# Fetching the condition indices as four packed rows and transposing them on VectorE, in a conditional FFN kernel

## The chip, the cores and the metric

The kernel runs on one core of a Trainium2 chip. The metric is the device time of one execution in microseconds (us), as the median of several runs. For the kernel before it is 79.45 us (three runs, 79.31 to 79.57). One more execution was recorded by the hardware profiler; all rows in this document come from such recordings. Engine names in rows: PE is TensorE's matmuls, PEld its weight loads, DVE is VectorE, ACT is ScalarE, POOL is GpSimd, and SPq is the queue on which SyncE issues DMAs.

## The reference, cut to what matters

```python
# x: (32, 32, 256) f32; conditions: (32,) int32; weights: (200, 32, 32)
w = weights[conditions]                          # one 32x32 matrix for each of 32 batches
y = jnp.einsum('bct,bcd->bdt', x, w)             # the mixing
h = jax.nn.silu(jnp.einsum('bsh,hi->bsi', y, w_gate)) * jnp.einsum('bsh,hi->bsi', y, w_up)
h_sparse = _sparsify_2to4(h)                     # keep the two largest of every four by magnitude
out = x + jnp.einsum('bsi,ih->bsh', h_sparse, w_down)
```

The condition index of each batch picks its 32x32 matrix. Nothing can be mixed, and so nothing can go through the FFN, before those matrices are on the chip.

## The kernel before, in words

The program is written engine by engine, with semaphores set by hand, so each engine does its work in the order of the code.

**The FFN.** 32 batches are handled in two halves of four groups, each group four batches on 128 partitions. A half has 512 columns, the intermediate dimension is 1024, taken in two quarters `q` of four 128-row tiles (`M = 4`). That gives 16 pairs of a gate product and an up product (`gate_up`, line 588, over `split_product`, line 564). Every f32 product is done as three products of a high and a low part, so six 128x512 matmuls per tile. The second matrix (`down`, line 599) follows at the end of TensorE's program. ScalarE makes the high parts, silu and magnitudes; VectorE makes the low parts, the gate times up products and the comparisons of the 2-in-4 selection.

**The start, which the change touches.** SyncE issues the small array `cond` first (line 189), then the first half of x (line 191) and the first gate weights (line 192). It then waits until the first gather has landed (line 194) before it issues the rest of the gate weights, the up weights and what follows. `cond` holds for each of the 128 partitions four int32: an index for each half, and for each half the first row of the partition's chunk in the table. The table is laid out by the host as 8 chunks of 200 rows, each row 128 floats. VectorE adds the two pairs (line 456), which gives `rows_sb`, one table row per partition and half. GpSimd, which has marked `own_block` by five small memsets before (lines 220 and 223), then runs two indirect DMAs (line 226), one per half, each of 128 rows of 512 bytes into `mix_row`. VectorE transposes the 32x32 blocks of the first (`transpose_rows`, line 365) and sets `transposed`.

TensorE in the meantime runs 12 matmuls on a constant whose result nobody uses (`warm_up`, line 533). It then waits for the first high gate weights, for `transposed` and for x (line 539), and mixes the first 128 features batch by batch in 32-row matmuls (line 544), the other 128 by a block-diagonal matrix in 128-row ones (line 558). `first_gates` (line 577, matmuls on line 585) and all the rest follow.

Of the kernel before, what the change touches and what calls it, by code (L numbers as in the profile page):

```python
# [10 lines left out]
def adaln_ffn(nc: bass.Bass, x: bass.AP, x_t: bass.AP, cond: bass.AP, table: bass.AP,  # L11
# [5 lines left out]
    f32 = mybir.dt.float32  # L17
    f32r = mybir.dt.float32r
    bf16 = mybir.dt.bfloat16
    ALU = mybir.AluOpType  # L20
    ACT = mybir.ActivationFunctionType

    P = 128
    i32 = mybir.dt.int32
    _, _, GH, T = x.shape
    NH = 2
    NG = NH * GH
    C = D = 32
    D4 = D // CHUNKS
    NB = P // C  # L30
# [17 lines left out]
    with ctx:  # L48
        def sb(name, shape, dt):
            return ctx.enter_context(nc.sbuf_tensor(name, shape, dt))  # L50

        def sem(name):
            return ctx.enter_context(nc.semaphore(name))

        x_sb = sb("x_sb", [P, NG, T], f32)
        cond_sb = sb("cond_sb", [P, 2 * NH], i32)
        rows_sb = sb("rows_sb", [P, NH], i32)
        raw_w = [sb("gate_raw", [P, NQ, KT, M * P], f32), sb("up_raw", [P, NQ, KT, M * P], f32)]
        down_raw = sb("down_raw", [P, NQ, M * T], f32)
        w_hl = [sb("gate_hl", [P, 2, NQ, KT, M, P], f32r), sb("up_hl", [P, 2, NQ, KT, M, P], f32r)]  # L60
# [43 lines left out]
            return (first_in[k], 16) if w == 0 else (up_in, 16)  # L104

        cond_in = sem("cond_in")
        x_in = [sem(f"x_in{i}") for i in range(NH)]
        up_in = sem("up_in")
        rest_in = [sem(f"rest_in{w}") for w in range(2)]
# [5 lines left out]
        rows_done = sem("rows_done")  # L115
        blocks_marked = sem("blocks_marked")
# [60 lines left out]
        def parts_until(u, j):  # L177
            return sum(len(p) for p in PARTS[:u]) + 1 + max(i for i, p in enumerate(PARTS[u]) if p[0] <= j)
# [7 lines left out]
            return w_hl[w][:, part, q, k:end, j:j_end]  # L186

        def sync_program(sp):
            sp.dma_start(cond_sb[:], cond).then_inc(cond_in, 16)

            sp.dma_start(x_sb[:, 0:GH, :], x[0]).then_inc(x_in[0], 16)
            sp.dma_start(raw_w[0][:, 0, 0, 0:2 * P], w_gate[0, 0, 0]).then_inc(first_in[0], 16)

            sp.wait_ge(mix_in[0], 16)
            for k in range(1, KT):
                sp.dma_start(raw_w[0][:, 0, k, 0:2 * P], w_gate[0, 0, k]).then_inc(first_in[k], 16)
            sp.dma_start(raw_w[1][:, 0, :, 0:2 * P], w_up[0, 0].rearrange("k p n -> p k n")).then_inc(up_in, 16)
            for w, weights in enumerate((w_gate, w_up)):
                sp.dma_start(raw_w[w][:, 0, :, 2 * P:4 * P],
                             weights[0, 1].rearrange("k p n -> p k n")).then_inc(rest_in[w], 16)  # L200
            sp.wait_ge(up_in, 16)
            sp.dma_start(x_sb[:, GH:NG, :], x[1]).then_inc(x_in[1], 16)
            for w, weights in enumerate((w_gate, w_up)):
                for i in range(2):
                    sp.dma_start(raw_w[w][:, 1, :, 2 * i * P:2 * (i + 1) * P],
                                 weights[1, i].rearrange("k p n -> p k n")).then_inc(second_in[w], 16)
            sp.dma_start(down_raw[:], w_down).then_inc(down_in, 16)
            sp.wait_ge(w_hi, GATE_PIECES_END)
            sp.wait_ge(w_lo, GATE_PIECES_END)
            sp.dma_start(xt_sb, x_t).then_inc(xt_in, 16)  # L210
            for i, (half, k, begin, end, _) in enumerate(OUTPUTS):
                if i not in (UNFINISHED, LEFT):
                    cols = slice(half * TH + begin, half * TH + end)
                    sp.wait_ge(out_done, i + 1)
                    sp.dma_start(out[:, k, cols], xt_sb[:, k, cols]).then_inc(stored, 16)

            sp.wait_ge(stored, 16 * (len(OUTPUTS) - 1))

        def gpsimd_program(pool):
            nc.gpsimd.memset(own_block[:], 0.0).then_inc(blocks_marked, 1)  # L220
            pool.wait_ge(blocks_marked, 1)
            for b in range(NB):
                nc.gpsimd.memset(own_block[b * C:(b + 1) * C, b:b + 1], 1.0).then_inc(blocks_marked, 1)
            pool.wait_ge(rows_done, 1)
            for half in range(NH):
                nc.gpsimd.indirect_dma_start(
                    out=mix_row[:, half], out_offset=None, in_=table,
                    in_offset=bass.IndirectOffsetOnAxis(ap=rows_sb[:, half:half + 1], axis=0),
                    engine_sem=gather_sent,
                ).then_inc(mix_in[half], 16)  # L230

            def low_down(q):
                pool.wait_ge(down_neg, q + 1)
                pool.dma_start(down_hl[:, LO, q].rearrange("p j t -> p (j t)"), down_raw[:, q],  # L234
                               accum_op=ALU.add).then_inc(down_lo_sent[q], 16)

            def low_h(u, j, end):
                pool.wait_ge(h_neg, parts_until(u, j))
                pool.dma_start(h_hl[:, u, LO, j:end], hs[u][:, j:end],  # L239
                               accum_op=ALU.add).then_inc(h_lo_sent[u][j // 2], 16)  # L240

            low_down(0)
            low_down(1)
            for u in range(SENT):
                for j, end in PARTS[u]:
                    low_h(u, j, end)
# [108 lines left out]
        def vector_program(dve):  # L355
# [9 lines left out]
            def transpose_rows(half):  # L365
                dve.wait_ge(mix_in[half], 16)
                groups = mix_w[:, half * GH:(half + 1) * GH].rearrange("p i o d -> p (i o d)")
                nc.vector.transpose(groups.rearrange("p (r e) -> p e r", e=D4),
                                    mix_row[:, half].rearrange("p (e c) -> p e c", e=D4)).then_inc(transposed, 1)
# [75 lines left out]
            def output(i):  # L445
# [3 lines left out]
                if i > UNFINISHED:  # L449
                    dve.wait_ge(out_done, UNFINISHED + 1)  # L450
                nc.vector.tensor_tensor(xt_sb[:, k, cols], bank[:, begin:end], xt_sb[:, k, cols],  # L451
                                        ALU.add).then_inc(out_done, 1)

            dve.wait_ge(cond_in, 16)
            dve.wait_ge(blocks_marked, 1 + NB)
            nc.vector.tensor_tensor(rows_sb[:], cond_sb[:, 0:NH], cond_sb[:, NH:2 * NH], ALU.add).then_inc(rows_done, 1)
            transpose_rows(0)
            diagonal(SPANS[0])
            diagonal(SPANS[1])
# [72 lines left out]
        def tensor_program(pe):  # L532
# [106 lines left out]
            for i in range(UNFINISHED + 1, len(OUTPUTS)):  # L639
                down(LAST, i, HALVED)  # L640

        sync_program(nc.sync)
        gpsimd_program(nc.gpsimd)
        scalar_program(nc.scalar)
        vector_program(nc.vector)
        tensor_program(nc.tensor)

# [47 lines left out]
```

## Time and profile before

| | |
|---|---|
| median of 3 runs | 79.45 us (79.31 to 79.57) |
| the profiled execution, its own time | 79.29 us |
| its span, first to last instruction | 78.0 us |
| PE busy | 74.8 us, 96% of the span |
| PEld busy | 59.7 us, 77% |
| DVE busy | 62.5 us, 80% |
| ACT busy | 42.1 us, 54% |
| POOL busy | 8.1 us, 10% |
| mean HBM and SBUF traffic | 124 GB/s |

The profiled execution's time is 1.29 us above its span: that is what lies before the first instruction and after the last. The profile gives a busy time per engine, the span in 40 equal slices, and a chain, followed back from the last instruction to what released each step. Matmuls are pipelined and their ends are modelled: a matmul's record is longer than the distance to the next one's start. An idle engine costs time only where another waits for it.

### The profile page before, as it was taken

What the parts mean: (1) busy time and instruction counts of PE and PEld (TensorE: products, weight loads), DVE (VectorE), ACT (ScalarE), POOL (GpSimd) and SP (SyncE); (2) the same over time, 40 slices, a digit from 0 to 9 for tenths busy, and PEclk for the clock granted to TensorE, in tenths of its full rate; (3) what the DMA queues carried; (4) which work ended last, traced back from release to release, by engine and by line L of the source; (5) the groups of instructions that cost most, each with busy time, mean ns of one, the idle gap of its engine ahead of it and who ended that gap; (6) DMA issues with size and microseconds to landing.
All of it is one profiled execution on the core that took longest, in us unless ns stands there. A gap on an engine that the chain in (4) does not pass through costs nothing.

```text
span 78.0 us, 1015 instructions
## 1 busy us (share of the span) xinstructions
PE 74.8 (96%) x362; PEld 59.7 (77%) x362; DVE 62.5 (80%) x92; ACT 42.1 (54%) x62; POOL 8.1 (10%) x17
## 2 busy tenths in 40 slices
PE   5999999999999999999999999999999999999970
PEld 2328888888888888888888888888888888888860
DVE  0016983699789999599999979999999999996370
ACT  6122863889443375599897759879380321830000
POOL 3550000000000013000713000005300000000000
PEclk9999999999999999999999999999999999999999
DMA  0836988997920004900099990001995000002534
GB/s 1 257 113 154 327 238 285 302 417 202 361 88 21 0 0 82 187 0 0 0 202 200 202 204 13 4 0 34 202 191 111 0 0 0 8 0 75 194 134 135
DMA packets 4566, 9.64 MB, mean 124 GB/s; under 512 B 561, under 2 KB 2865, under 8 KB 4305
## 3 DMA queue, kind: packets, MB, share of 16 engines
q1 hardware_dynamic: 3488, 6.16, 23.5%
q0 software_dynamic: 928, 3.28, 22.1%
q10 hardware_dynamic: 144, 0.13, 0.5%
q8 instruction: 3, 0.05, 0.3%
q14 instruction: 3, 0.02, 0.1%
HBM read 5.38 MB, written 1.05 MB: 82 GB/s over the span
## 4 chain that ended last, share of the span: by engine, by line
PE 96%; DVE 1%; issue 0%
PE banks L573 52%; PE banks L615 28%; PE banks L535 7%; PE banks L558 4%; PE banks L585 4%; PE banks L544 1%; DVE gate_raw L451 1%
## 5 line engine op out<-in xcount | busy, mean ns | idle before, releaser
L573 PE MATMUL banks<-y_hl,up_hl 128*128 128x512 f32 x96 | 24.2, 389 | 0.0
L615 PE MATMUL banks<-h_hl,down_hl 128*128 128x512 f32 (+1 forms) x102 | 22.0, 376 | 0.0
L573 PE MATMUL banks<-y_hl,gate_hl 128*128 128x512 f32 x84 | 21.4, 390 | 0.0
L615 PEld LDWEIGHTS banks<-h_hl,down_hl 128*128 128x128 f32 x102 | 18.5, 188 | 3.6
L573 PEld LDWEIGHTS banks<-y_hl,up_hl 128*128 128x128 f32 x96 | 18.0, 188 | 3.7
L573 PEld LDWEIGHTS banks<-y_hl,gate_hl 128*128 128x128 f32 x84 | 15.7, 188 | 3.2
L262 ACT ACTIVATE silu<-banks 128x512 f32<-128x512 f32 x16 | 9.6, 597 | 11.4 <-PE banks L573 11.1
L400 DVE TENSOR_TENSOR h<-banks,silu 128x512 f32<-128x512 f32 x12 | 8.2, 687 | 4.0 <-ACT silu L262 3.9
L283 ACT ACTIVATE h_hl<-h 128x1024 fp32r<-128x1024 f32 (+1 forms) x8 | 6.7, 842 | 3.9 <-DVE h L436 3.9
L436 DVE SCALAR_TENSOR_TENSOR h<-count,h 128x512 f32<-128x512 bf16 x12 | 7.9, 685 | 0.1
L535 PE MATMUL banks<-const-bfloat16-1.0 128*128 128x512 bf16 x12 | 5.3, 627 | 0.8 <-PEq L684 0.8
L269 ACT ACTIVATE x_sb<-h 128x512 f32<-128x512 f32 x8 | 4.9, 625 | 1.7 <-DVE h L400 1.7
L451 DVE TENSOR_TENSOR gate_raw<-banks,gate_raw 128x512 f32<-128x512 f32 (+1 forms) x6 | 3.5, 599 | 2.4 <-PE banks L615 2.3
L239 POOL DMA_DIRECT2D h_hl<-h x4 | 3.7, 930 | 13.4 <-ACT h_hl L287 13.4
L234 POOL DMA_DIRECT2D down_hl<-down_raw x2 | 1.8, 920 | 31.3 <-ACT down_hl L278 31.3
L411 DVE TENSOR_TENSOR far<-x_sb 128x1024 bf16<-128x1024 f32 x4 | 4.9, 1221 | 0.2
L411 DVE TENSOR_TENSOR far<-a_even 128x1024 bf16<-128x1024 f32 x4 | 4.9, 1220 | 0.2
L535 PEld LDWEIGHTS banks<-const-bfloat16-1.0 128*128 128x128 bf16 x12 | 1.6, 140 | 3.5 <-issue 3.5
L252 ACT ACTIVATE gate_hl<-gate_raw 128x256 fp32r<-128x256 f32 (+2 forms) x4 | 2.5, 630 | 3.2 <-DMA gate_raw<-in_w_gate 3.1
L287 ACT ACTIVATE h_hl<-h 128x1024 fp32r<-128x1024 f32 x4 | 4.2, 1054 | 0.0
L283 ACT ACTIVATE h_hl<-up_raw 128x1024 fp32r<-128x1024 f32 x2 | 2.1, 1054 | 3.2 <-DVE up_raw L436 3.2
L389 DVE TENSOR_TENSOR y_hl<-banks,y_hl 128x512 fp32r<-128x512 f32 (+1 forms) x3 | 2.6, 867 | 0.9 <-ACT y_hl L256 0.8
(38 smaller groups left out, 66.2 us busy)
## 6 DMA issues: line engine op xcount, KB each, us to landing
h_hl<-h POOLq DMA_DIRECT2D x4, 512.0 KB, 6.1
x_sb<-in_x SPq DMA_DIRECT2D x2, 512.0 KB, 4.3
up_raw<-in_w_up SPq DMA_DIRECT2D x4, 256.0 KB, 4.5
down_raw<-in_w_down SPq DMA_DIRECT2D x1, 1024.0 KB, 8.0
gate_raw<-in_x_t SPq DMA_DIRECT2D x1, 1024.0 KB, 7.3
down_hl<-down_raw POOLq DMA_DIRECT2D x2, 512.0 KB, 4.8
gate_raw<-in_w_gate SPq DMA_DIRECT2D x3, 256.0 KB, 4.2
out<-gate_raw SPq DMA_DIRECT2D x3, 256.0 KB, 2.3
```

What stands on the lines that cost most here:

```text
L239: pool.dma_start(h_hl[:, u, LO, j:end], hs[u][:, j:end], accum_op=ALU.add).then_inc(h_lo_sent[u][j // 2], 16)
L262: nc.scalar.activation(silu[:, n % 3], gate_bank(n), ACT.Silu).then_inc(silu_done, 1)
L269: nc.scalar.activation(a[u % 2][:, j], hs[u][:, j], ACT.Abs).then_inc(abs_done, 1)
L283: nc.scalar.activation(h_hl[:, u, HI, j:end], hs[u][:, j:end], ACT.Copy).then_inc(h_hi, 1)
L287: nc.scalar.activation(h_hl[:, u, LO, j:end], hs[u][:, j:end], ACT.Copy, scale=-1.0).then_inc(h_neg, 1)
L400: nc.vector.tensor_tensor(hs[u][:, j], up_bank(n), silu[:, n % 3], ALU.mult).then_inc(h_done, 1)
L411: step(nc.vector.tensor_tensor(far[:, j - 2::2], au[:, 0:2], au[:, j:j + 1].broadcast_to([P, 2, TH]), ALU.is_ge))
L436: nc.vector.scalar_tensor_tensor(hs[u][:, j], count[:, j], bound, hs[u][:, j], op, ALU.mult).then_inc(masked, 1)
L451: nc.vector.tensor_tensor(xt_sb[:, k, cols], bank[:, begin:end], xt_sb[:, k, cols], ALU.add).then_inc(out_done, 1)
L535: nc.tensor.matmul(gate_bank(0), ones[:, 0:P], ones, start=True, stop=True)
L573: last = nc.tensor.matmul(dst, w_hl[w][:, s, q, k, j], y_hl[:, m, half, k], start=i == 0, stop=i == len(terms) - 1)
L615: last = nc.tensor.matmul(bank[:, begin:end], down_hl[:, s, q, j, k * P:(k + 1) * P], h_hl[:, u, m, j, begin:end], start=(q, j, m, s) == f ...
```

## The change

The host now packs `cond` into four rows, one for each group of 32 partitions: 32 indices of the first half, 32 of the second, and 32 first rows of chunks, 96 int32 (384 bytes) per row. The DMA writes them to partitions 0, 32, 64 and 96. As the other partitions of that tile would hold what was there before, VectorE first clears the whole tile, and SyncE waits for that before it issues any DMA. When the rows are in, VectorE adds the first rows to both halves' indices (64 sums per partition, of which only those on the four partitions mean something), waits for the sums, and transposes a 128x32 tile of them per half in 32x32 blocks, so that column 0 of each block column holds the table row of each partition. GpSimd waits for each half's transpose before that half's gather.

```diff
-        cond_sb = sb("cond_sb", [P, 2 * NH], i32)
-        rows_sb = sb("rows_sb", [P, NH], i32)
+        cond_sb = sb("cond_sb", [P, (NH + 1) * C], i32)
+        sums_sb = sb("sums_sb", [P, NH * C], i32)
+        rows_sb = sb("rows_sb", [P, NH * C], f32)
...
         def sync_program(sp):
-            sp.dma_start(cond_sb[:], cond).then_inc(cond_in, 16)
+            sp.wait_ge(cond_clear, 1)
+            sp.dma_start(cond_sb[0:P:C], cond).then_inc(cond_in, 16)
 
             sp.dma_start(x_sb[:, 0:GH, :], x[0]).then_inc(x_in[0], 16)
...
-            pool.wait_ge(rows_done, 1)
             for half in range(NH):
+                pool.wait_ge(rows_done, half + 1)
                 nc.gpsimd.indirect_dma_start(
                     out=mix_row[:, half], out_offset=None, in_=table,
-                    in_offset=bass.IndirectOffsetOnAxis(ap=rows_sb[:, half:half + 1], axis=0),
+                    in_offset=bass.IndirectOffsetOnAxis(ap=rows_sb[:, half * C:half * C + 1].bitcast(i32), axis=0),
...
+            nc.vector.memset(cond_sb[:], 0).then_inc(cond_clear, 1)
+            dve.wait_ge(blocks_marked, 1 + NB)
             dve.wait_ge(cond_in, 16)
-            dve.wait_ge(blocks_marked, 1 + NB)
-            nc.vector.tensor_tensor(rows_sb[:], cond_sb[:, 0:NH], cond_sb[:, NH:2 * NH], ALU.add).then_inc(rows_done, 1)
+            halves = cond_sb.rearrange("p (f r) -> p f r", r=C)
+            nc.vector.tensor_tensor(sums_sb.rearrange("p (f r) -> p f r", r=C), halves[:, 0:NH],
+                                    halves[:, NH:NH + 1].broadcast_to([P, NH, C]), ALU.add).then_inc(rows_summed, 1)
+            dve.wait_ge(rows_summed, 1)
+            for half in range(NH):
+                nc.vector.transpose(rows_sb[:, half * C:(half + 1) * C],
+                                    sums_sb[:, half * C:(half + 1) * C].bitcast(f32)).then_inc(rows_done, 1)
             transpose_rows(0)
...
-    cond = _np.concatenate([cond, first], axis=-1).reshape(P, 2 * NH)
+    cond = _np.concatenate([cond, first[..., :1]], axis=-1).reshape(NB, P // NB, NH + 1).transpose(0, 2, 1).reshape(NB, -1)
```

VectorE's queue at the start of the program, before: the ISA row is the add of the indices, the STREAM_TRANSPOSE the one of the gathered rows.

```order
L456 ISA rows_sb<-cond_sb 128x4 [waits barrier_Pool_Activation_PE_DVE_SP_release,blocks_marked,cond_in]
L368 STREAM_TRANSPOSE h<-h 128x4x32 [waits mix_in0]
L376 TENSOR_TENSOR h<-h,own_block 128x256 [waits transposed] x2
L382 TENSOR_TENSOR gate_hl<-gate_raw,gate_hl 128x256 [waits first_in0,w_hi]
L389 TENSOR_TENSOR y_hl<-banks,y_hl 128x512 [waits mixed,y_hi]
```

And the same place in the change, where the first line of the gathered rows is L373:

```order
L459 MEMSET cond_sb 128x96 [waits barrier_Pool_Activation_PE_DVE_SP_release]
L463 ISA sums_sb<-cond_sb 128x128 [waits cond_in,blocks_marked]
L467 STREAM_TRANSPOSE rows_sb<-sums_sb 128x32 [waits rows_summed]
L467 STREAM_TRANSPOSE rows_sb<-sums_sb 128x32
L373 STREAM_TRANSPOSE h<-h 128x4x32 [waits mix_in0]
L381 TENSOR_TENSOR h<-h,own_block 128x256 [waits transposed] x2
```

One instruction has become four: a clear ahead of the load, a wider add, and two transposes behind it. (The add is shown in 16-bit words, two for each int32, which is how the profile counts it too.)

SyncE's queue at the start of the program in the change:

```order
L194 DMA cond_sb<-in_cond 4x96 [waits barrier_Pool_Activation_PE_DVE_SP_release,cond_clear]
L196 DMA x_sb<-in_x 128x1024
L197 DMA gate_raw<-in_w_gate 128x256
L201 DMA gate_raw<-in_w_gate 128x256 [waits mix_in0]
L202 DMA up_raw<-in_w_up 128x2x256
```

The order of the DMAs is the old one. The first now waits for VectorE's clear, and with it the two behind it that waited for nothing; it has 4 rows of 96 elements where it had 128 rows of 4.

## Rows read from the trace of the kernel before

**Rows 1.** The page: busy time and share by engine; slices of PE busy.

```profile
PE 74.8 (96%) x362; PEld 59.7 (77%) x362; DVE 62.5 (80%) x92; ACT 42.1 (54%) x62; POOL 8.1 (10%) x17
...
PE   5999999999999999999999999999999999999970
```

**Rows 2.** The chain in order of time: start us, us, what.

```profile
0.79 5.28 PE banks L535 x12
6.07 0.01 issue
6.08 1.17 PE banks L544 x32
7.24 1.09 PE banks L558 x8
8.33 2.75 PE banks L585 x12
...
53.77 21.84 PE banks L615 x102
75.61 0.02 issue
75.63 0.42 DVE gate_raw L451
```

**Rows 3.** Timeline of PE and PEld near 6 us: start, us, engine, line, operation.

```profile
5.43 0.63 PE L535 MATMUL banks<-const-bfloat16-1.0 128*128 128x512 bf16 x1
...
6.04 0.31 PEld L544 LDWEIGHTS banks<-h,x_sb 32*128 32x128 f32 x4 [0.89 <-ACT gate_hl L252]
```

**Rows 4.** Timeline of DVE from 0.5 to 6.2 us.

```profile
2.40 0.16 DVE L456 CUSTOM_DVE_ANT_0 rows_sb<-cond_sb 128x4 uint16<-128x4 uint16 x1 [2.40 <-DMA cond_sb<-in_cond]
5.57 0.40 DVE L368 STREAM_TRANSPOSE h<-h 128x128 f32<-128x128 f32 x1 [3.02 <-DMA h<-in_table,rows_sb]
6.01 0.42 DVE L376 TENSOR_TENSOR h<-h,own_block 128x256 f32<-128x256 f32 x1
```

**Rows 5.** Timeline of POOL from 0.5 to 6.2 us.

```profile
0.75 0.10 POOL L220 MEMSET own_block<- 128x4 f32 x1 [0.29 <-POOLq L684]
0.91 0.53 POOL L223 MEMSET own_block<- 32x1 f32 x4
2.85 1.19 POOL L226 DMA_INDIRECT h<-in_table,rows_sb  x1 [1.41 <-DVE rows_sb L456]
4.34 1.00 POOL L226 DMA_INDIRECT h<-in_table,rows_sb  x1 [0.30 <-issue]
```

**Rows 6.** Timeline of SyncE's queue, and ScalarE's first weights.

```profile
0.75 0.38 SPq L189 DMA_DIRECT2D cond_sb<-in_cond  x1
1.19 0.42 SPq L191 DMA_DIRECT2D x_sb<-in_x  x1
...
5.12 0.42 ACT L252 ACTIVATE gate_hl<-gate_raw 128x256 fp32r<-128x256 f32 x1 [2.88 <-DMA gate_raw<-in_w_gate]
```

**Rows 7.** Stretches: us, length, granted clock, DMA share, GB/s.

```profile
1.70:2.05 0.35, 1.00 0.21 6
2.05:2.20 0.15, 1.00 0.00 0
...
4.70:5.00 0.30, 1.00 0.86 222
5.00:5.50 0.50, 1.00 0.01 0
```

**Rows 8.** VectorE's groups by form: busy us, mean ns of one, idle before.

```profile
L382 DVE TENSOR_TENSOR gate_hl<-gate_raw,gate_hl 128x512 fp32r<-128x512 f32 x1 | 0.7, 693 | 0.0
L376 DVE TENSOR_TENSOR h<-h,own_block 128x256 f32<-128x256 f32 x2 | 0.8, 421 | 0.0
```

**Rows 9.** Timeline of the end: an add on VectorE and the store it releases.

```profile
72.84 0.69 DVE L451 TENSOR_TENSOR gate_raw<-banks,gate_raw 128x512 f32<-128x512 f32 x1 [1.38 <-PE banks L615]
73.56 2.85 SPq L215 DMA_DIRECT2D out<-gate_raw  x2
```

**Rows 10.** Instructions of x_sb in 6.05 to 6.3, then 6.6 to 7.0: ns min/median/max.

```profile
L544 PE MATMUL banks<-h,x_sb x6: 271/365/374, 6.1 to 6.3; 32*128 32x32 f32 x6
...
L544 PE MATMUL banks<-h,x_sb x24: 271/271/271, 6.4 to 7.0; 32*128 32x32 f32 x24
```

More of the change, by code:

```diff
@@ L106, in adaln_ffn @@
         cond_in = sem("cond_in")
+        cond_clear = sem("cond_clear")
+        rows_summed = sem("rows_summed")
         x_in = [sem(f"x_in{i}") for i in range(NH)]
```

## The prediction

> **What bounds the kernel now.** I read the page first: TensorE is busy for 96% of the span, and full from the second slice to the second last [rows 1]. The chain of waits in order of time says the same more sharply: from 0.79 us to 75.61 it is TensorE alone, with no step of another engine in between [rows 2]. So nothing that VectorE, SyncE or GpSimd does is paid for, unless it moves a moment at which TensorE starts; and a moment once moved is never won back, since no idle time follows that could absorb it.
>
> One such moment matters here: the first useful matmul, at 6.08 us. The chain puts the 12 warm-up matmuls in front of it, as if they set it [rows 2]. The timeline around 6 us says more. The last warm-up matmul starts at 5.43 and its record ends near 6.07; but records are longer than the distance between starts, which is 5.28 / 12 = 0.44 us here, so TensorE could have taken the next one at about 5.87. The first weight load of the mixing starts at 6.04 [rows 3]. VectorE's transpose of the gathered rows ends at 5.57 + 0.40 = 5.97 [rows 4]. The load comes 0.07 us behind it. The other two conditions were met earlier: the high weights end at 5.12 + 0.42 = 5.54 [rows 6], and the load traffic of x is over by 5.00 us [rows 7]. So the start is set by the gather's chain: cond lands, VectorE adds (2.40 to 2.56), GpSimd takes up the gather at 2.85 and needs 1.19 us to issue it [rows 4, 5], its data move between 4.70 and 5.00 [rows 7], and VectorE sees them at 5.57 [rows 4]. There is no slack to cover a delay of this chain, at most 0.03 us to the end of the warm-up's record, which I count as nothing. An earlier end would gain up to about 0.2 us (6.08 less 5.87), and not more.
>
> **The change, part by part.** It lengthens or shortens this one chain.
>
> 1. *The clear, ahead of the load.* cond is issued at 0.75 us, as soon as the program starts [rows 6]. Now VectorE must write 128x96 words first. No memset of VectorE's is in the trace. GpSimd's of 128x4 takes 0.10 us [rows 5], a lower bound. VectorE's two-operand instructions take 421 ns at 256 elements and 693 at 512, so 1.06 ns per element on top of 149 ns [rows 8]; 96 elements by that line give 0.25, the upper bound. Between these, with the add of four elements at 0.16 us nearby [rows 4], I take 0.17.
> 2. *SyncE's new wait.* VectorE's add at the end finishes at 73.53 and the store it releases is issued at 73.56 [rows 9]: 0.03 us. Steps 1 and 2 together move three DMAs by 0.20 us: cond, and behind it x and the first gate weights. The latter two are covered: ScalarE's first weights would end at 5.74 instead of 5.54, and x's traffic at 5.20 instead of 5.00, both ahead of the 6.04 that they would have to pass. GpSimd's memsets end at 1.44 [rows 5], long before cond lands, so swapping the two waits costs nothing.
> 3. *The load itself.* Its 128 packets of 16 bytes move from 1.70 to 2.05 us, at 6 GB/s and a DMA share of 0.21 [rows 7]: the time goes into their number, not their bytes. Four packets of 384 bytes should need little of these 0.35 us. Bounds: a gain of 0.35, and none. I take 0.25, as the engines start one after another during most of that stretch while the first byte still has to come. The 0.95 us before and the 0.35 us behind (to 2.40) are round trips that I leave alone.
> 4. *The wider add.* 128 words of 16 bits in place of 4. At 1.06 ns for each of 124 more [rows 8] it costs 0.13 us. Bounds: 0, if the form of the operands doesn't matter at this size, and 0.26, twice the rate, as this is a custom operation with one measurement only.
> 5. *VectorE's wait for its own sums.* The transpose of the gathered rows ends at 5.97 and the multiply that waits for it starts at 6.01 [rows 4]: 0.04 us.
> 6. *The first transpose.* 128 elements per partition take 0.40 us [rows 4]; this one has 32. In proportion that is 0.10, the lower bound. With the 149 ns of rows 8 as the fixed part, (404 - 149) / 4 more gives 0.21; with one element per 1.06 ns and all the rest fixed, 0.30, the upper bound. I take 0.21, for the fixed part is what VectorE's other rows share.
> 7. *The second transpose and the second wait of GpSimd.* GpSimd spends 1.19 us on the first gather and takes up the second at 4.34 [rows 5], so a second transpose that ends 0.2 us behind the first is free. The second gather's rows, later by the same delay as the first's, are wanted only at the second half's mixing, many matmuls on. Nothing.
>
> A rule of the Trainium skill bears on step 6: "Vector Engine (DVE) Microarchitecture Reference", section 3.8 on the reshape front-end, has the transpose fill an array and drain it at a sustained rate of one element per cycle and lane. The measured 0.40 us for 128 elements does not say how it splits. By that rule the 0.30 of the upper bound would be right, and the sum 0.09 us larger.
>
> Sum: 0.17 + 0.03 - 0.25 + 0.13 + 0.04 + 0.21 = **+0.33 us**. Everything behind hangs on the gather's landing or on TensorE itself (SyncE issues the rest of the gate weights and the up weights when the gather has landed), so it moves along as a block. TensorE pauses before 6.08 us for 0.2 us now, and would for 0.5. Of the profiled execution that makes 79.29 + 0.33 = 79.62, of the median 79.45 + 0.33 = **79.78 us**. The profiled execution lies 0.16 below the median and within 0.02 of the lowest run; a difference carries over. The bounds give 0.10 + 0.03 - 0.35 + 0 + 0.04 + 0.10 = -0.08, so 79.37, and 0.25 + 0.03 - 0 + 0.26 + 0.04 + 0.30 = +0.88, so 80.33.
>
> **The rivals.**
>
> *The smaller load buys nothing (80.03).* The landing may be set by round trips, with the packets' 0.35 us hidden in them: then step 3 is 0 and the sum is +0.58. For it: the traffic is only 0.35 of the 1.65 us between issue and use, and VectorE starts 0.35 us after it is over. Against it: a landing waits for the last packet, and the last one moves at 2.05. The Trainium skill, "DMA: Bandwidth & Descriptors", section on the anatomy of one DMA, speaks for this rival: it calls the fixed cost constant, and says that many descriptors can be emitted before their number shows.
>
> *Not slower (79.50).* The landing gains its full 0.35 us, clear and transpose cost their lower bounds of 0.10 each: 0.10 + 0.03 - 0.35 + 0.13 + 0.04 + 0.10 = +0.05. The place is the cond load, the price the 0.35; it decides once landing and transpose together are at least 0.10 us better than I took them, which puts the sum under 0.24. For it: four packets are as few as it gets, and the transposed tile is a single block wide. Against it: VectorE's shortest recorded instruction, with four elements, takes 0.16 us, so 0.10 for a transpose would be out of line.
>
> *TensorE stays at its low clock for longer (80.87).* The granted clock reads 1.00 in all stretches [rows 7], but the warm-up's 512 columns take 0.44 us, which is the 1.2 GHz level, and a first-gate matmul of as many 2.75 / 12 = 0.23 us, the 2.4 GHz level [rows 2]. The records of the mixing's first six matmuls go up to 374 ns, from 6.4 us on all take 271 [rows 10]: the rise falls at about 6.3 us, after five microseconds of matmuls back to back. A pause that is 0.33 us longer lies just before it. If it put the rise off past the mixing, the 128-row matmuls would take up to twice their 1.09 us [rows 2]: 79.45 + 0.33 + 1.09 = 80.87. The Trainium skill, "TensorE: Matmul & The Clock Gate", Part 1, has activity release the throttle, at a moment that varies from run to run. Against it: TensorE already pauses 0.2 us there, and the rise came all the same.
>
> *Faster.* At most 0.2 us are to be won before the warm-up itself binds, less than a measurement can tell; only a rise of the clock that falls earlier could add to it. That the change does something other than it says I see no room for: the order of instructions shows all its parts.
>
> **How the numbers follow.** Forecast 0.45, the useless smaller load 0.23, not slower 0.23, low clock 0.05, faster 0.04. A measurement of this kernel can tell 0.3%, or 0.24 us, from no change. Of the forecast's 0.45 I put 0.12 below 0.24 us, as its own range is about 79.6 to 79.95. Slower: 0.33 + 0.23 + 0.05 = 0.61. Same: 0.23 + 0.12 = 0.35. Faster: 0.04. The range goes from 79.40, just under the rival that isn't slower, to 80.15, above the useless smaller load; beyond lie the low clock and the far ends of the bounds.
>
> **What would show it right or wrong.** Right: a memset of about 0.17 us on VectorE from 0.75; cond issued at 0.95; the add starting near 2.35; the first gather taken up near 3.2 instead of 2.85; the first load of the mixing near 6.37 instead of 6.04; and from there a chain of TensorE alone, of the old length. Step 3 is wrong if the add still starts 1.65 us after cond's issue. Steps 4 and 6 are read from their own rows. The whole is wrong if the first load of the mixing has not moved by what the total has, for then time came or went behind it.

## The result and the profile after

The changed kernel takes 80.39 us (median of 7 executions, 80.27 to 83.42) where the kernel before takes 79.45 (7 executions, 79.21 to 81.25). The ratio is 1.0122, with a 95% interval of 1.0104 to 1.0139: slower by about 0.97 us. The forecast was 79.78 with a range of 79.40 to 80.15, so the sign was right and the time outside the range. The ratio leaves out executions in which TensorE's granted clock falls to half for some microseconds; the profiled execution of the changed kernel (83.42 us, span 82.1) is one of them, so its rows show the later start and, on top, such a fall.

The chain of waits of the changed kernel, in order of time (start us, us, what):

```profile
0.84 0.15 DVE cond_sb L459
0.99 0.02 issue
1.01 1.78 DMA cond_sb<-in_cond
2.79 0.03 issue
2.82 0.02 DVEq L461
2.84 0.09 issue
2.93 0.24 DVE sums_sb L463
3.16 0.02 issue
3.19 0.32 DVE rows_sb L467 x2
3.50 0.19 issue
3.69 2.81 DMA h<-in_table,rows_sb
6.50 0.02 issue
6.52 0.41 DVE h L373
6.93 0.09 issue
7.03 1.52 PE banks L556 x32
8.55 2.00 PE banks L570 x8
10.55 4.57 PE banks L597 x12
15.13 5.47 PE banks L585 x24
```

Before, the chain was TensorE alone [rows 2]. Now its first seven microseconds are the fetching of the indices and matrices: clear, load, add, transposes, gather, transpose. The two queue entries that changed most, from its timeline:

```profile
1.01 0.65 SPq L194 DMA_DIRECT2D cond_sb<-in_cond  x1
...
3.69 1.19 POOL L231 DMA_INDIRECT h<-in_table,rows_sb  x1 [2.26 <-DVE rows_sb L467]
...
7.00 1.42 PEld L556 LDWEIGHTS banks<-h,x_sb 32*128 32x128 f32 x32 [2.32 <-issue]
```

The small load takes SyncE 0.65 us to issue, where the 128-row one took 0.38 [rows 6]. The gather is taken up at 3.69 instead of 2.85 [rows 5], and the first weight load of the mixing starts at 7.00 instead of 6.04 [rows 3]: 0.96 us, the whole difference that the ratio gives.

TensorE's stretches of the same execution (us, length, PE busy, granted clock, DMA share, GB/s):

```profile
6.00:7.00 1.00, 0.00 (x0) 1.00 0.15 45
7.00:8.00 1.00, 0.97 (x28) 0.76 0.39 103
8.00:9.00 1.00, 1.00 (x14) 0.50 0.77 242
...
14.00:15.00 1.00, 1.00 (x5) 0.83 0.94 297
```

The warm-up ended at 0.79 + 4.38 = 5.17 us, earlier than before (6.07), since the clock had risen earlier; TensorE then stood still for 1.86 us. The granted clock fell from 1.00 to 0.50, which is the 1.2 GHz level, soon after the mixing had begun, and stayed there until past 14 us. Mixing and first gates took 1.52 + 2.00 + 4.57 = 8.09 us in the chain, against 1.17 + 1.09 + 2.75 = 5.01 before [rows 2]: 3.08 us more. 0.96 + 3.08 makes 4.04 us, which is the difference of the spans (82.1 against 78.0) within rounding. So there are two effects, a certain one of 0.96 us and an occasional one. The kernel before has the second as well: over all comparisons here 8 of its 46 executions took 80.88 us or more.

### The profile page after: what moved, and what is told of

It reads as the page before. It is cut to its first block, busy times and chain, and to the rows that moved or that the text cites. A ratio compares the mean times of both kernels' runs of the same rounds, so it can differ in the third digit from the quotient of the medians.

```text
span 82.1 us, 1018 instructions
## 1 busy us (share of the span) xinstructions
PE 77.0 (94%) x362; PEld 62.1 (76%) x362; DVE 62.7 (76%) x95; ACT 41.6 (51%) x62; POOL 8.1 (10%) x17
## 4 chain that ended last, share of the span: by engine, by line
PE 89%; DMA 6%; DVE 2%; issue 1%; DVEq 0%
PE banks L585 50%; PE banks L627 27%; PE banks L597 6%; PE banks L570 5%; DMA h<-in_table,rows_sb 3%; DMA cond_sb<-in_cond 2%; PE banks L556 2%; DVE gate_raw L456 1%; DVE h L373 1%; DVE rows_sb L467 0%; DVE sums_sb L463 0%; DVE cond_sb L459 0%; DVEq L461 0%
## 5 line engine op out<-in xcount | busy, mean ns | idle before, releaser
L585 PE MATMUL banks<-y_hl,up_hl 128*128 128x512 f32 x96 | 24.2, 389 | 0.0
L585 PE MATMUL banks<-y_hl,gate_hl 128*128 128x512 f32 x84 | 21.4, 390 | 0.0
L585 PEld LDWEIGHTS banks<-y_hl,up_hl 128*128 128x128 f32 x96 | 18.0, 188 | 3.8
L585 PEld LDWEIGHTS banks<-y_hl,gate_hl 128*128 128x128 f32 x84 | 15.7, 188 | 3.2
L547 PE MATMUL banks<-const-bfloat16-1.0 128*128 128x512 bf16 x12 | 4.4, 539 | 0.8 <-PEq L696 0.8
L597 PE MATMUL banks<-y_hl,gate_hl 128*128 128x512 f32 x12 | 4.9, 588 | 0.0
L597 PEld LDWEIGHTS banks<-y_hl,gate_hl 128*128 128x128 f32 x12 | 3.6, 313 | 0.9
L261 ACT ACTIVATE y_hl<-banks 128x512 fp32r<-128x512 f32 (+1 forms) x3 | 2.2, 737 | 3.8 <-PE banks L556 2.7
```

The lines of the kernel that those rows point to most:

```text
L547: nc.tensor.matmul(gate_bank(0), ones[:, 0:P], ones, start=True, stop=True)
L585: last = nc.tensor.matmul(dst, w_hl[w][:, s, q, k, j], y_hl[:, m, half, k], start=i == 0, stop=i == len(terms) - 1)
L597: nc.tensor.matmul(gate_bank(n), w_hl[0][:, s, 0, k, n], y_hl[:, m, 0, k], start=i == 0, stop=i == len(terms) - 1)
```

## The experiments

Each was timed beside the kernel before on the same chip; where a ratio is given it has the same meaning as above, but for experiment 9, as said there. A number in brackets behind a ratio is its 95% interval. "The fall" is the fall of TensorE's granted clock to 0.50.

**1. The changed kernel again.** No edit.

> The changed kernel again, for a second profile. In the first one the cond load of 4 rows was issued at 1.01 us, took SyncE 0.65 us to issue (0.38 before), and VectorE's add started 1.92 us after the issue (1.65 before). Theory A (the 4-row form is dear to issue and so lands later): the same numbers again, 0.63 to 0.67 and 1.9, and the median near 80.3. Rival B (it was an accident of that execution): issue near 0.4, add 1.65 behind it, and a median near 79.9. On the clock: the first profile has TensorE without work from 5.2 to 7.0 us and the granted clock at 0.50 from about 7.8 to 14.2 us. If such a fall belongs to the pause, it is seen again in some executions; the remaining ones differ from the kernel before by the later first weight load alone (7.0 against 6.04), so by 0.9 to 1.0 us.

Six executions: 80.40, 81.79, 81.80, 81.92, 83.42, 83.68. So it was no accident: five show the fall of the clock, and the one that doesn't is at 80.4. From the timeline:

```profile
1.01 0.65 SPq L194 DMA_DIRECT2D cond_sb<-in_cond  x1
...
2.95 0.23 DVE L463 CUSTOM_DVE_ANT_0 sums_sb<-cond_sb 128x128 uint16<-128x128 uint16 x1 [1.97 <-DMA cond_sb<-in_cond]
```

Theory A holds within 0.02 us: 0.65 us to issue, the add 1.94 us behind it, where it was 1.92. The fall is there again, but shorter. From the chain, and TensorE's stretches as above:

```profile
0.79 5.16 PE banks L547 x12
5.95 1.02 issue
...
9.00:10.00 1.00, 1.00 (x5) 0.55 1.05 349
```

TensorE paused for 1.02 us, worked for two more at a granted clock of 1.00, and the clock was down from 9 us to past 12, half as long as in the first profile. That fits the two levels of the longer executions, near 81.8 (this profile's is 81.79) and near 83.4 (the first one's is 83.42).

**2. The clear alone.**

```diff
+        clear_sb = sb("clear_sb", [P, 96], i32)
...
+            sp.wait_ge(cond_clear, 1)
             sp.dma_start(cond_sb[:], cond).then_inc(cond_in, 16)
...
+            nc.vector.memset(clear_sb[:], 0).then_inc(cond_clear, 1)
             dve.wait_ge(cond_in, 16)
```

> The kernel before, with only the clear of a 128x96 tile on VectorE ahead of the first DMA and SyncE's wait for it. Theory A (the shape of the 4-row load costs, not the wait): cond is issued near 1.01 us instead of 0.75 and takes 0.38 us to issue as before; the add starts 1.65 us later, near 2.66, the first load of the mixing near 6.30, and the time is 0.26 us over before, 79.7. Rival B (a DMA that is issued right behind a semaphore wait is slow to issue, whatever its shape): issue takes about 0.65 us here too, the add starts near 2.93, and the time is 0.5 us over before, 79.95.

Four executions of 79.55 to 79.70 and one of 81.27; ratio 1.0032 (1.0018 to 1.0045), or 0.25 us. From the timeline of the one at 81.27:

```profile
1.00 0.38 SPq L192 DMA_DIRECT2D cond_sb<-in_cond  x1
...
2.77 0.16 DVE L460 CUSTOM_DVE_ANT_0 rows_sb<-cond_sb 128x4 uint16<-128x4 uint16 x1 [1.79 <-DMA cond_sb<-in_cond]
```

`clear_sb` is a 128x96 tile of its own, of which nothing is read. The DMA behind a wait is issued in 0.38 us as ever: rival B is out, and steps 1 and 2 of the prediction are worth 0.25 us in the executions without the fall. The profile has one miss: the add starts 1.77 us behind the issue and not 1.65, so the landing of one and the same load varies by 0.1 us between profiles.

**3. Sixteen rows.**

```diff
-            sp.dma_start(cond_sb[0:P:C], cond).then_inc(cond_in, 16)
+            sp.dma_start(cond_sb[0:P:8], cond).then_inc(cond_in, 16)
```

The host sends each row four times (`.repeat(4, axis=0)` behind its packing of `cond`).

> The changed kernel, but cond is sent as 16 rows of 384 bytes to every 8th partition; the twelve extra rows are never used. Theory A (a load that is spread over 4 of the 16 DMA engines is what is dear): issue falls from 0.65 to about 0.40 us, the add starts near 1.01 + 1.45 = 2.46 to 2.6 us, and the time falls from 80.3 to about 79.9. Rival B (rows on distant partitions, or the 384-byte row, are what is dear): issue stays near 0.65, the add near 2.93, the time at 80.3.

Six executions, 80.26, and five of 81.75 to 83.55. From the timeline:

```profile
1.00 0.58 SPq L194 DMA_DIRECT2D cond_sb<-in_cond  x1
...
3.06 0.22 DVE L463 CUSTOM_DVE_ANT_0 sums_sb<-cond_sb 128x128 uint16<-128x128 uint16 x1 [2.08 <-DMA cond_sb<-in_cond]
```

Theory A in this form, that a load of only four rows, spread over few DMA engines, is the trouble, fell (no view here shows the engines one by one). Four times as many rows are issued barely faster, and the add comes later still. What the two loads share is that they step over partitions.

**4. All 128 rows, no clear.**

```diff
-            sp.wait_ge(cond_clear, 1)
-            sp.dma_start(cond_sb[0:P:C], cond).then_inc(cond_in, 16)
+            sp.dma_start(cond_sb[:], cond).then_inc(cond_in, 16)
...
-            nc.vector.memset(cond_sb[:], 0).then_inc(cond_clear, 1)
```

The host sends each row 32 times (`.repeat(32, axis=0)`).

> The changed kernel, but the host sends each of the four rows 32 times, so that the load fills all 128 partitions with 384 bytes each; the clear and SyncE's wait for it go away. What is left of the change is the wider add, VectorE's wait for its own sums and the first transpose. By the rows of the changed kernel these take from 2.93 to 3.40, 0.47 us, where the add alone took 0.16: 0.31 us more. Theory A: cond issued at 0.75 with 0.38 us, the add at 2.40 to 2.45, the gather taken up near 3.16 to 3.2, the first load of the mixing near 6.37, the time 0.33 over before, 79.8. Rival C (TensorE has slack that the first profile hides): the time stays within 0.1 of 79.45.

Without the fall 79.90 and 80.03, with it 81.42 to 83.05; ratio 1.0077 (1.0059 to 1.0095), or 0.61 us. From the timeline:

```profile
0.75 0.38 SPq L192 DMA_DIRECT2D cond_sb<-in_cond  x1
...
2.64 0.23 DVE L460 CUSTOM_DVE_ANT_0 sums_sb<-cond_sb 128x128 uint16<-128x128 uint16 x1 [2.64 <-DMA cond_sb<-in_cond]
```

128 rows on neighbouring partitions are issued in 0.38 us though they hold 24 times the bytes of the kernel before. The add starts 0.24 us later than before, which I had not expected; its rows of 384 bytes keep the traffic until 2.15 us instead of 2.05. The time is longer all the same, so there is no slack, and rival C is out.

**5. Four rows on neighbouring partitions.**

```diff
-            sp.dma_start(cond_sb[0:P:C], cond).then_inc(cond_in, 16)
+            sp.dma_start(cond_sb[0:4], cond).then_inc(cond_in, 16)
```

This leaves out the rows of partitions 32, 64 and 96, so most indices are zero and the output isn't the kernel's; only its times are of use.

> The changed kernel, with the four rows written to partitions 0 to 3 instead of 0, 32, 64 and 96, for the time alone: the indices that the gather gets are then mostly zero, so it fetches mostly one row of the table. Theory F (a destination that steps over partitions is what is dear to issue: 0.65 us with a step of 32, 0.58 with a step of 8, 0.38 for all 128 in a row): the issue takes about 0.38 us, the add starts about 0.3 us earlier than 2.93, and executions without a fall of the clock take 80.0. Rival G (few rows, on fewer than all engines, are what is dear): the issue stays at 0.65 and the time at 80.3. The gather from one row could itself be faster or slower; that is read apart, from its issue to its landing.

From its timeline, its chain, and the stretch of the load's traffic (as in [rows 7]):

```profile
1.01 0.37 SPq L194 DMA_DIRECT2D cond_sb<-in_cond  x1
...
2.65 0.23 DVE L463 CUSTOM_DVE_ANT_0 sums_sb<-cond_sb 128x128 uint16<-128x128 uint16 x1 [1.67 <-DMA cond_sb<-in_cond]
...
1.01 1.50 DMA cond_sb<-in_cond
...
3.41 3.48 DMA h<-in_table,rows_sb
...
1.90:2.20 0.30, 1.00 0.03 5
```

Theory F is right and G wrong: the same four packets of 384 bytes are issued in 0.37 us, and the add starts at 2.65 instead of 2.93. The step over partitions costs 0.28 us, issue and start alike. The total (82.01 to 83.45) says nothing on this: all five executions had the fall. The gather of mostly one and the same row took from 3.41 to 6.92 us, 3.51 where other gathers take some 2.8, and so made the pause longer, 2.57 us in the profile.

**6. VectorE's waits in the old order.**

```diff
-            dve.wait_ge(blocks_marked, 1 + NB)
             dve.wait_ge(cond_in, 16)
+            dve.wait_ge(blocks_marked, 1 + NB)
```

> The changed kernel with VectorE's two waits in the old order, first for cond and then for GpSimd's marks, which are set at 1.44 us. In the changed kernel the chain of waits has 0.14 us from cond's landing (2.79) to the add (2.93), with a queue entry of VectorE and 0.09 us of issue between; with the old order in the clear-only kernel it has 0.02 (2.75 to 2.77). Theory H (the wait that comes last in time must be the one attached to the instruction, else its start costs 0.1 us more): it is the other way round than one would think, so the add starts 0.02 to 0.03 behind the landing here and the time falls by 0.1 us, to 80.2. Rival I (the 0.14 belongs to the four-row load or to the wide add): 0.14 again, 80.3.

Without the fall 80.01, 80.11 and 80.18 (three with it, 81.71 to 81.81); ratio 1.0086 (1.006 to 1.0112), which overlaps the change's own. The add in the timeline:

```profile
2.82 0.23 DVE L463 CUSTOM_DVE_ANT_0 sums_sb<-cond_sb 128x128 uint16<-128x128 uint16 x1 [1.84 <-DMA cond_sb<-in_cond]
```

The add starts 1.81 us behind the issue. In the three profiles of the same load with the new order it is 1.92, 1.94 and, in experiment 8 below, 2.03: 0.11 to 0.22 less, which is the way theory H has it. But these three differ among themselves by as much as H claims, so a part may be the landing itself, and experiment 7 speaks against H.

**7. All rows and the old order of the waits.** The edits of 4 and 6 together.

> The kernel of the experiment in which all 128 partitions are loaded with 384 bytes and the clear is gone, now with VectorE's waits in the old order (cond first, GpSimd's marks attached to the add). There the add started at 2.64 us, 1.89 behind the issue, and executions whose clock stayed up took 79.9 to 80.0. By theory H the order is worth 0.1 us: the add starts near 2.53, the gather is taken up near 3.3, the time is 79.8. What is then left over the kernel before is the wider add, the own wait and the transpose (0.31 us) and what the bigger load lands later. If the order is worth nothing here (rival I), the add stays at 2.64 and the time at 79.95.

Five executions of 79.72 to 79.94 and one of 83.01; ratio 1.0066 (1.0053 to 1.008), or 0.52 us. But the add starts at 2.63, where it was 2.64 with the other order, so rival I has the rows here and H only a time that lies within the other interval. What the order of waits is worth, nothing or some 0.1 us, stays open. One execution of six had the fall, where it was four of six in experiment 4; in this profile the pause is 0.64 us, in that one 1.63.

**8. Sixteen warm-up matmuls** in the changed kernel (`WARM_START = 16`).

> The changed kernel with 16 warm-up matmuls instead of 12. The gather's chain is untouched, so the first weight load of the mixing stays near 6.95 to 7.0 us. Theory D (the granted clock falls to 0.50 because TensorE stood without work for 1.0 to 1.9 us before the mixing): the four matmuls take 0.44 us each at the low level and 0.22 at the high one, so the pause shrinks by 0.9 to 1.7 us; the fall at 7.8 or 9.1 us is gone or rarer, and the median over all executions goes from 81.9 down to the 80.3 to 80.4 of the executions without a fall. Rival E (the fall has to do with the 32-row mixing matmuls, or comes at random): the granted clock still reads 0.50 between 8 and 14 us in about half of the executions. If the warm-up now ends too late, the mixing starts at the end of the warm-up's last matmul, at up to 7.3 us, and the time is up to 0.3 us longer.

Five executions, 80.13 to 80.41, none longer; ratio 1.0111 (1.009 to 1.0132). The chain in order of time:

```profile
0.79 5.72 PE banks L547 x16
6.51 0.60 issue
7.11 1.09 PE banks L556 x32
8.20 1.09 PE banks L570 x8
9.29 2.77 PE banks L597 x12
```

The start is as late as in the changed kernel, but the pause is 0.60 us and the granted clock stays at 1.00. The falls, in 8 of 13 executions with 12 matmuls, are gone. The later start remains, and with it 0.88 us of time by the ratio: filling a pause doesn't bring the start forward.

**9. Ten warm-up matmuls in the kernel before** (`WARM_START = 10`, in place of 12), which lengthens the pause and touches nothing else.

> The kernel before with 10 warm-up matmuls instead of 12, so that TensorE pauses for some 0.9 us more ahead of a mixing that starts at the same time. Theory D (a longer pause makes the granted clock fall to 0.50 afterwards): the fall is seen in more executions than in the kernel before's own (4 of the last 11 were 1.5 us longer), so the median of all lies near 81 or shows values of 80.9 to 81.1 in half or more; the others stay at 79.4. Rival E (the fall comes at random): as rarely as before.

All five executions take 80.92 to 81.07 us, all at a mean granted clock of 0.975 to 0.979, so all with the fall. The ratio of 1.0209 (1.0196 to 1.0222) therefore sets executions with the fall against those of the kernel before without it, and is the price of the fall. The mixing and first gates in its chain:

```profile
6.21 1.09 PE banks L544 x32
7.31 1.67 PE banks L558 x8
8.98 3.76 PE banks L585 x12
```

The load at the start of the same chain, which is the old one, for comparison with experiment 5:

```profile
0.75 1.62 DMA cond_sb<-in_cond
```

And TensorE's stretches (us, length, PE busy, granted clock, DMA share, GB/s):

```profile
7.00:8.00 1.00, 1.00 (x17) 0.82 0.72 234
8.00:9.00 1.00, 1.00 (x6) 0.50 1.10 363
...
11.00:12.00 1.00, 1.00 (x6) 0.98 0.91 344
```

Two matmuls whose result nobody uses are worth 1.65 us (medians 80.96 and 79.31): the warm-up ends at 4.79, TensorE stands still for 1.42 us, the mixing starts only 0.13 later than in [rows 2], and yet 128-row mixing and first gates take 1.67 + 3.76 instead of 1.09 + 2.75. Rival E is out; this is the clearest evidence for theory D, as nothing of the change is in it.

**10. Fourteen warm-up matmuls in the kernel before.**

> The kernel before with 14 warm-up matmuls. The gather's chain lets the mixing start near 6.05 us. If the clock rises as late as in the first profile (about 6.3 us), matmul 13 takes 0.44 and 14 0.22 us or so, and the mixing starts near 6.5, so the time is 0.4 us longer: 79.8. If it rises earlier (4.2 to 5.6 us in other profiles), the warm-up ends before 6.05 and the time is 79.4. Theory D: no execution of 80.9 or more, as hardly a pause is left. Rival E: some of 81 all the same.

Twelve executions from 79.19 to 80.07, median 79.46, none with the fall; the kernel before beside it has a median of 79.31 over 17, one of them at 81.18. Ratio 1.0021 (0.9998 to 1.0044). That agrees with theory D but is weak evidence, as only one in 17 of the kernel before beside it had the fall. Its interval reaches from no loss to 0.35 us. The price in single executions is as expected: where the clock rises late, the warm-up itself is in the way (in the profiled execution, 79.92 us, it lasts from 0.79 to 6.73).

**11. The repaired idea.** All rows, no clear, old order of waits, 14 warm-up matmuls.

> All 128 partitions loaded, no clear, old order of the waits, and 14 warm-up matmuls: the idea of the change with its three dear places mended. Theories A, F, H and D together: the mixing starts near 6.5 us, set by the gather or by the warm-up, whichever is later; all executions take 79.8 to 79.9 and none shows the fall of the clock. It would still be 0.4 us behind the kernel before where that one's clock stays up, and 1.1 ahead of it where it falls. If the fall still comes with this short pause, theory D is too simple.

Six executions, 79.64 to 80.16, median 79.89; ratio 1.0068 (1.0049 to 1.0087). By the ratios it is 0.4 us better than the change without the fall and still 0.5 behind the kernel before, and no better than experiment 7 with its 12 matmuls (1.0066). What it adds is that none of its executions had the fall; the pause is 0.88 us in the profile.

**12. The add on GpSimd,** an attempt to shorten the old chain.

```diff
+            pool.wait_ge(blocks_marked, 1 + NB)
+            pool.wait_ge(cond_in, 16)
+            nc.gpsimd.tensor_tensor(rows_sb[:], cond_sb[:, 0:NH], cond_sb[:, NH:2 * NH], ALU.add).then_inc(rows_done, 1)
             pool.wait_ge(rows_done, 1)
...
-            dve.wait_ge(cond_in, 16)
             dve.wait_ge(blocks_marked, 1 + NB)
-            nc.vector.tensor_tensor(rows_sb[:], cond_sb[:, 0:NH], cond_sb[:, NH:2 * NH], ALU.add).then_inc(rows_done, 1)
```

> The kernel before, with the add of the two columns moved from VectorE to GpSimd, which needs the sums: an attempt to shorten the chain that the change lengthens. VectorE's add takes 0.16 us and GpSimd takes up the gather 0.29 us behind it, 0.45 us from cond's use at 2.40 to 2.85. On GpSimd a small memset takes 0.10 us, and waiting for its own result about as long as VectorE's own wait, 0.04 to 0.1. Theory J (TensorE's start follows the gather's chain down to 5.87 us): the gather is taken up near 2.65, the mixing's first weight load near 5.84 to 5.9, and the time falls by 0.1 to 0.2 us, to 79.3. Rival K (the end of the warm-up binds as well): the gather is earlier and the time stays at 79.4.

GpSimd in the timeline:

```profile
2.78 0.19 POOL L226 TENSOR_TENSOR rows_sb<-cond_sb 128x2 int32<-128x2 int32 x1 [1.34 <-DMA cond_sb<-in_cond]
3.59 1.20 POOL L229 DMA_INDIRECT h<-in_table,rows_sb  x1 [0.62 <-POOL rows_sb L226]
```

Both theories missed: the add starts at 2.78 instead of 2.40, and the gather is taken up 0.81 us after the add's start, where it was 0.45. Not all of the first is GpSimd's: the load is put down as landed 1.9 us behind its issue here and 1.6 before. Nor is the profiled execution (80.16) a typical one; it is the longest of six from 79.74 on. Ratio 1.0061 (1.004 to 1.0083). No version that was run beats the kernel before.

## Why the prediction was wrong where it was

**What bounds.** Right. The gather's chain sets TensorE's start, there is no slack, and what moves the start is paid in full: 0.96 us of start for 0.97 of time. From the 24 up-product matmuls behind the first gates on (L585 x24, 5.47 us), the pieces of the chain are those of before.

**Steps 1 and 2, clear and wait: 0.20 forecast, 0.26 measured** (cond issued at 1.01 instead of 0.75). The memset takes 0.15 in the chain; I had left out that VectorE's first instruction starts at 0.84 and not at 0.75. That x and the first gate weights are covered held: ScalarE's first weights weren't what the mixing waited for.

**Step 3, the load: 0.25 gained forecast, 0.27 lost measured.** This is the step that failed, by 0.52 us, and its bounds (a gain of 0.35, or none) didn't hold it. These are two stretches of the changed kernel around the load's traffic (us, length, granted clock, DMA share, GB/s):

```profile
2.30:2.50 0.20, 1.00 0.04 8
2.50:2.70 0.20, 1.00 0.00 0
```

The four packets are over within 0.2 us, where 128 took 0.35 [rows 7]. But "the 0.95 us before" that I left alone became about 1.3: the issue alone grew from 0.38 to 0.65. Experiment 5 shows the cause: the destination that steps over 32 partitions, not the number of rows. It shows too that the gain itself was sized too high. Without the step the load lands 1.50 us behind its issue, against 1.62 for the old one (experiment 9) and 1.74 in experiment 2: 0.12 us gained, at most 0.24. And "the time goes into their number" isn't borne out: the traffic of four packets to neighbouring partitions still takes 0.30 us (1.90 to 2.20), that of 128 rows of the same 384 bytes some 0.40 (1.75 to 2.15 in experiment 4). Beyond that, about 0.1 us went between landing and add: 0.14 here, 0.03 in experiment 9. Whether by the order of the waits is open (experiments 6 and 7). So the 0.27 is 0.28 for the step, less 0.12 for the packets, plus 0.11 behind the landing, with one or two profiles behind each and a scatter of 0.1 us in the landing. I had excluded a loss without a reason: no row of the trace had a DMA of this shape, so the bounds should have been open towards a loss. That DMA engines start one after another, my reason for 0.25, no view here shows.

**Step 4, the add: 0.13 forecast, 0.07 measured** (226 ns against 160). **Step 5, the own wait: 0.04 forecast, 0.03 measured. Step 6, the transpose: 0.21 forecast, 0.21 measured.** The new transposes, ns min/median/max, first and last start:

```profile
L467 DVE STREAM_TRANSPOSE rows_sb<-sums_sb x2: 169/190/211, 3.2 to 3.3; 128x32 f32<-128x32 f32 x2
```

This speaks against the rule of the Trainium skill that I had weighed ("Vector Engine (DVE) Microarchitecture Reference", section 3.8), for f32 elements at least: 128 elements take 404 ns and the first transpose of 32 takes 211, so 96 more elements cost 2.0 ns each. One element per cycle, which I had taken as 1.06 ns each and which gave 0.30, isn't what this transpose shows. **Step 7** held: the first gather is taken up 0.29 us behind the first transpose's end as before behind the add, and the second transpose delays nothing.

Steps 1 to 6 as measured make 0.26 + 0.27 + 0.07 + 0.03 + 0.21 = 0.84, the move of the gather from 2.85 to 3.69. The gather itself took 0.11 us longer to be seen in this profile, 0.03 in that of experiment 1; with 0.01 behind it that makes the 0.96 us of the start.

**The rivals.** The useless smaller load (80.03) was nearest in time, and for four rows on neighbouring partitions it is nearly what the runs show: 1.64 us from issue to add in experiment 5, against 1.65 before. What it lacked as well is the 0.28 us that the step over partitions costs. The section of the Trainium skill that speaks for it in the prediction is about DMAs that GpSimd issues; this one is SyncE's. The low clock, given 0.05 and 80.87 us, was too low in both. I had it as a later rise; it is a fall after the rise, seen in 8 of 13 executions of the change, at 1.4 to 3.3 us each, and the price of doubled 128-row matmuls left out the first gates (4.57 us instead of 2.75). The Trainium skill's "TensorE: Matmul & The Clock Gate", Part 1, agrees on the point that the moment of the rise varies from run to run: the warm-up's 12 matmuls end between 4.85 (experiment 5) and 6.07 us here, and so the pause behind them varies for one and the same kernel. I had taken the one profile's warm-up as that of all executions, though the kernel before has falls of its own.

## What to carry to other kernels

Price a DMA of a new shape by its issue as well as by its packets, and where no row of the trace has the shape, leave its price open towards a loss: 124 packets fewer brought the landing some 0.12 us forward, and the step over partitions that bought it cost 0.28. Where a chain sets an engine's start, count the extra instructions of a clever layout in that chain, since here each 0.03 to 0.26 us was paid in full. When a start moves later, look at what the pause does to TensorE's clock over many executions, not in one profile, and try a longer warm-up: four more matmuls took the falls away here, though not the later start.

## What the runs showed of the hardware

- SyncE issues a load of four 384-byte rows in 0.37 us to partitions 0 to 3 and in 0.65 to every 32nd (four profiles); sixteen rows to every 8th take 0.58, 128 neighbouring rows 0.38. Why the step costs this is not shown.
- Two f32 transposes of 128x32 on VectorE, one behind the other, took 211 and 169 ns, one of 128x128 404.
- A pause of 1.42 us in TensorE's work ahead of the mixing (experiment 9) was followed by a granted clock of 0.50 until about 11 us in the profile, and all five executions had the fall. Pauses of 0.60 to 0.93 us in four profiles (experiments 7, 8, 11 and 12) were not followed by it, those of 1.02 us (experiments 1 and 6), 1.12 (experiment 3), and 1.43 to 2.57 (experiments 2, 4, 5 and the first profile) were. The moment at which the warm-up ended doesn't part them: it is 5.97 in experiment 7, without the fall, and 5.95 in experiment 1, with it. Whether the length of the pause alone decides is open.
- An indirect DMA of 128 times mostly the same table row took 3.51 us from its start to its use (one profile, experiment 5), against 2.7 to 2.9 in the other profiles.
- GpSimd's add of 128x2 int32 took 0.19 us, and 0.62 us passed (one profile, experiment 12) before the indirect DMA that waited for it was taken up; behind VectorE's add it was 0.29.
